# Attention with layer norm: three of the four statistics of a coming group taken in the group's first tile

## The chip, the core and the metric

The kernel runs on one core of one Trainium2 chip. The core has five engines that run side by side and meet only at semaphores: PE (matrix products, the loads of its weights shown apart as PEld), DVE (vector work), ACT (activations and copies), POOL (vector work too), and SP, which here issues the transfers. The metric is the device time of one execution in microseconds (us), lower is better.

## What is computed

A block of a transformer over 8192 rows of 512 numbers, in single precision: layer norm with a modulation, causal linear attention with 16 heads, a gated residual, then a second layer norm with a modulation, a gated feed-forward with 1536 hidden columns, and a gated residual. The change is in the attention half:

```python
h = _layernorm(x) * (1 + ca) + sa          # x is (1, 8192, 512)
qkv = h @ W_qkv + b_qkv                    # q, k, v; 16 heads of 32
q = elu(q * E ** -0.5) + EPS_FEAT
k = elu(k) + EPS_FEAT
kv_s = kv_s + einsum('bhe,bhf->bhef', k_t, v_t)     # per row t, carried on
k_s = k_s + k_t
out_t = einsum('bhe,bhef->bhf', q_t, kv_s) / (einsum('bhe,bhe->bh', q_t, k_s) + EPS_DEN)
x = x + ga * (out @ W_out + b_out)
```

The layer norm needs the mean and the variance of each row of 512.

## The kernel before

Each engine has its own program, written out by hand; the order of the work on an engine is the order of the calls, and every dependency is a wait on a semaphore (`wait`). There is no scheduler. Rows are handled in tiles of 128 and groups of 4 tiles, 16 groups in all. Groups 0 and 1 are written out, groups 2 to 13 run in a loop whose body holds an even and an odd group (`groups`), groups 14 and 15 are written out again. One body works on three groups at once: in group g it computes the attention of the four tiles of g, the projections and features of g + 1, and the layer norm and turning of g + 2.

The program of DVE for groups 0 to 14 is `ahead_of_last`. In it, for each tile t of group g:

- `mask`: four operations that multiply PE's scores in `sc` by the causal mask and write `probs`.
- `feature(n, ...)`: adds the two parts of the feature map (`z_relu`, `z_exp`, from ACT); for a key also a scan, which gives `k_sum`, and a copy of its last column.
- `gate_last`: writes `y`, the gated output product of the tile before, from PE's bank.
- `divide`: numerators from two PSUM banks (`num` and `pj`) times the reciprocal denominators, written to `a_t` in two halves. It releases `a_ready`.
- `norm_stats`, `norm_var`, `norm_x`: the layer norm of group g + 2. `norm_stats` waits for the load of `xg`, 128 rows x 4 tiles x 512, and takes one statistics instruction for each tile; `norm_var` merges them into mean and variance and writes `var_eps`; POOL turns this into `rstd`; `norm_x` normalises `xg` in place.
- `word_size`: only in looped groups; the largest absolute value of a block of feed-forward weights (`most`), merged into `most_of_all` by an operation of one element in each partition.

PE (`front` and `rest`) starts each tile with the scores and three products of 12 matmuls (a product is three passes of four matmuls of 128x512). Two of them wait on semaphores that matter here: in `front`, `wait(pe, a_ready, g * GT + t)` stands in front of the second product of a tile, since that product writes into the bank which `divide` of the tile before reads. The output product (`out_project`, into `sc`) of the tile before follows in `rest`. In group 14 (`near_last`) PE also waits, in `scores` of the second tile, for a flag `wide` that DVE writes behind `divide` of the first tile.

POOL works on the same groups: in tile 1 of a group its queue has `prod_low` (`prod_lo`), a bias add into `x_res`, `rstd_of`, a product `prod` from `k_sum` and `qt`, and the residual add into `x_res`, which waits for `y`. ACT computes the exponentials and the copies. SP loads `xg` of group g + 2 early in group g.

Of the kernel before, what the change touches and what calls it, by code (L numbers as in the profile page):

```python
# [23 lines left out]
GT = 4  # L24
# [24 lines left out]
def wait(eng, sem, value):  # L49

    if not isinstance(value, int) or value > 0:
        eng.wait_ge(sem, value)  # L52
# [127 lines left out]
def attention(nc, s, sem, sbuf, psum, ident, gb_dram, mod_col, half_neg, w_hi, w_lo, xt_hi, xt_lo, ga_row,  # L180
# [100 lines left out]
    def odd_bank(tile, t):  # L281

        if isinstance(tile, int) and tile >= (NG - 1) * GT:
            return turn_bank_of(tile) if t < 3 else sc[:, 0, :]
        return pj[:, (t + 1) % 2, :]
# [554 lines left out]
    def vector(dve, sum_of, low):  # L840
        def norm_stats(g, tiles=range(GT)):
            wait(dve, x_in, 16 * (g + 1))
            for t in tiles:
                ins = dve.bn_stats(stats[:, t, :], xg[:, t, :])
            if tiles[-1] == GT - 1:
                ins.then_inc(ln_chain, 1)

        def norm_var(g):
            wait(dve, ln_chain, 2 * g + 1)
            wait(dve, xn_ready, g)  # L850
            if not isinstance(g, int):
                dve.sem_inc(dve_passed, 1)
            for t in range(GT):
                ins = dve.bn_aggr(mean_var[:, t, :], stats[:, t, :])
            ins.then_inc(ln_chain, 1)
            wait(dve, ln_chain, 2 * g + 2)
            dve.tensor_scalar(var_eps[:, 0:GT], mean_var[:, 0:GT, 1], EPS_LN, None, ALU.add).then_inc(var_ready, 1)
# [21 lines left out]
        def feature(g, parity, n):  # L879

            kind, c = unit_of(n)
            to = (kt, qt)[kind][parity]
            wait(dve, exp_ready, g * 2 * C + n + 1)
            dve.scalar_tensor_tensor(to[:, c, :], z_relu[:, n % 2, :], EPS_FEAT, z_exp[:, n % 2, :],
                                     ALU.add, ALU.add).then_inc(phi_ready, 1)
            if kind == 0:
                wait(dve, phi_ready, g * 2 * C + n + 1)
                wait(dve, prod_ready, g * C + c - 1)
                first = isinstance(g, int) and g == 0
                wait(dve, past_ready, (g - 1) * C + c + 1)  # L890
                dve.tensor_tensor_scan(k_sum[:, c % 2, :], to[:, c, :], to[:, c, :],
                                       0.0 if first else k_past[:, c:c + 1],
                                       ALU.add, ALU.bypass).then_inc(ksum_ready, 1)
                wait(dve, ksum_ready, g * C + c + 1)
                dve.tensor_copy(k_past[:, c:c + 1], k_sum[:, c % 2, GN - 1:GN]).then_inc(past_ready, 1)

        def v_rows(g, parity, t):
            wait(dve, pj_ready, g * UNITS + 2 * C + t + 1)
            dve.tensor_tensor(out=v[parity][:, t, :], in0=pj[:, t % 2, :], in1=bv_row[:, :],
                              op=ALU.add).then_inc(v_ready, 1)  # L900

        def recip(g, parity, c):
            wait(dve, den_ready, g * C + c + 1)
            dve.reciprocal(r_den[parity][:, c, :], r_den[parity][:, c, :]).then_inc(rden_ready, 1)  # L904

        def mask(tile):
            wait(dve, sc_ready, tile + 1)
            for h in range(HPC):
                dve.tensor_tensor(out=probs[:, h, :].rearrange("p (c i) -> p c i", c=C),  # L909
                                  in0=sc[:, h, :].rearrange("p (c i) -> p c i", c=C),  # L910
                                  in1=causal[:, :].rearrange("p (a i) -> p a i", a=1).broadcast_to([P, C, P]),
                                  op=ALU.mult).then_inc(probs_ready, 1)

        def divide(tile, g, parity, t):
            wait(dve, num_ready, tile + 1)
            wait(dve, rden_ready, (g + 1) * C)
            wait(dve, a_lo_ready, tile)
            for odd, bank in enumerate((num, odd_bank(tile, t))):
                ins = dve.tensor_tensor(out=a_t[:, :].rearrange("p (k e i) -> p e k i", e=2, k=2)[:, odd, :, :],  # L919
                                        in0=bank[:, :].rearrange("p (k e i) -> p e k i", e=2, k=2)[:, odd, :, :],  # L920
                                        in1=r_den[parity][:, :, t * P:(t + 1) * P]
                                        .rearrange("p (k e) i -> p e k i", e=2)[:, odd, :, :], op=ALU.mult)
            ins.then_inc(a_ready, 1)

        def gate_y(tile):
            wait(dve, op_ready, tile + 1)
            if isinstance(tile, int) and tile == 0:
                dve.wait_ge(ga_ready, 2)
            wait(dve, y_ready, tile)
            dve.tensor_tensor(out=y[:, :], in0=y_bank_of(tile), in1=ga_row[:, :],  # L930
                              op=ALU.mult).then_inc(y_gated, 1)

        def gate_last(g, t):
            tile = g * GT + t - 1
            if not isinstance(tile, int) or tile >= 0:
                gate_y(tile)

        def word_size(i, slot, words, landed):

            wait(dve, *landed)  # L940
            dve.tensor_reduce(most[:, slot:slot + 1], words.bitcast(I32), AX.X, ALU.max,
                              apply_absolute_value=True).then_inc(most_ready, 1)
            wait(dve, most_ready, i + 2)
            wait(dve, most_merged, i + 1)
            dve.tensor_tensor(out=most_of_all[:, :], in0=most_of_all[:, :], in1=most[:, slot:slot + 1],
                              op=ALU.max).then_inc(most_merged, 1)
# [78 lines left out]
        def ahead_of_last(g, parity):  # L1025
            n = g + 1
            other = 1 - parity
            looped = not isinstance(g, int)
            near_last = isinstance(g, int) and g == NG - 2
            first = isinstance(g, int) and g == 0  # L1030

            mask(g * GT)
            if not first:
                v_rows(g, parity, 3)
                recip(g, parity, 3)
            feature(n, other, 0)
            if first:
                recip(0, 0, 2)
                recip(0, 0, 3)
            feature(n, other, 1)  # L1040
            gate_last(g, 0)
            divide(g * GT, g, parity, 0)
            if near_last:
                dve.wait_ge(beyond_ps, 1)
                dve.tensor_scalar(wide[:, :], x_bank[0:1, 0:1], 0.5, None, ALU.is_gt).then_inc(wide_ready, 1)

            mask(g * GT + 1)
            norm_stats(g + 2)
            norm_var(g + 2)
            feature(n, other, 2)  # L1050
            feature(n, other, 3)
            if looped:
                word_size(g * 3 + (-6), 0, r_den[other][:, 2, :], (unit_in[0], g * 16 + (-16)))
            gate_last(g, 1)
            if looped:
                word_size(g * 3 + (-5), 1, r_den[other][:, 1, :], (down_in, g * 16 + (-16)))
            feature(n, other, 4)
            norm_x(g + 2)
            divide(g * GT + 1, g, parity, 1)

            mask(g * GT + 2)
            feature(n, other, 5)
            recip(n, other, 0)
            feature(n, other, 6)
            xt_low(g + 2, parity, 0)
            feature(n, other, 7)
            gate_last(g, 2)
            if looped:
                word_size(g * 3 + (-4), 2, r_den[other][:, 3, :], (unit_in[1], g * 16 + (-16)))
            divide(g * GT + 2, g, parity, 2)  # L1070
            xt_low(g + 2, parity, 1)

            mask(g * GT + 3)
            v_rows(n, other, 0)
            recip(n, other, 1)
            v_rows(n, other, 1)
            xt_low(g + 2, parity, 2)
            v_rows(n, other, 2)
            if near_last:
                recip(n, other, 2)  # L1080
            gate_last(g, 3)
            if not near_last:
                recip(n, other, 2)
            xt_low(g + 2, parity, 3)
            divide(g * GT + 3, g, parity, 3)

        def group(g, parity):
# [10 lines left out]
            if not last:  # L1098
                return ahead_of_last(g, parity)
# [1103 lines left out]
```

## Time and profile before

| what | us |
|---|---|
| median of 3 runs | 2059.73 |
| lowest and highest run | 2059.23 and 2059.74 |
| the profiled execution | 2060.73 |
| its span | 2059.0 |
| granted clock of PE over the span | 0.998 of full speed |

The rows further down come from the profiled execution. The attention part takes about the first 1050 us of it, a looped group 63 us, a tile 15 to 17 us. All looped groups look alike; group 7, whose four tiles start near 515, 530, 545 and 561 us, is the one from which single rows are read.

### The profile page before, as it was taken

The page shows a single profiled execution, that of the slowest core. Times are in us where ns is not written, and L with a number is a line of the kernel's source. Part 1 is how long each engine was busy: PE and PEld are TensorE (multiplying, and loading weights), DVE is VectorE, ACT ScalarE, POOL GpSimd, SP SyncE. Part 2 cuts the span into 40 slices and gives each one's busy share as a digit, 9 for nine tenths or more (in the row PEclk, how much of TensorE's full clock was granted, in tenths as well). Part 3 has the DMA queues.
Part 4 walks back from the last instruction along what each step waited for, and adds up shares of the span by engine and source line. Part 5 has one row for each costly group of instructions (what it writes and reads, how often), then busy time and mean ns, then how long its engine had stood idle before and what let it go on. Part 6 is the DMA issues. An engine that isn't in the chain of part 4 may idle for free. (4 is left out here: it accounts for less than half of the span.)

```text
span 2059.0 us, 44446 instructions
## 1 busy us (share of the span) xinstructions
PE 2021.3 (98%) x16388; PEld 1645.8 (80%) x16388; DVE 1554.2 (75%) x2228; ACT 1001.7 (49%) x1733; POOL 956.9 (46%) x782
## 2 busy tenths in 40 slices
PE   7999999999999999999999999999999999999998
PEld 4788888888888888888868888888888888878887
DVE  7988988898988899888885755857567575765743
ACT  5444554555544455545453544535464353644533
POOL 2645544555445455444534344443534444344444
PEclk9999999999999999999999999999999999999999
DMA  7111222321222322222266465654646556465453
GB/s 260 32 58 47 79 83 88 98 93 58 90 91 83 99 68 80 85 89 83 73 221 224 150 204 184 204 183 168 194 168 208 179 177 204 143 215 178 163 169 103
DMA packets 157163, 276.80 MB, mean 134 GB/s; under 512 B 11105, under 2 KB 35681, under 8 KB 157026
## 3 DMA queue, kind: packets, MB, share of 16 engines
q1 hardware_dynamic: 156498, 273.73, 40.4%
q8 instruction: 110, 1.80, 0.4%
q10 hardware_dynamic: 528, 1.05, 0.1%
q14 instruction: 27, 0.22, 0.0%
HBM read 208.67 MB, written 66.06 MB: 133 GB/s over the span
## 5 line engine op out<-in xcount | busy, mean ns | idle before, releaser
L1639 POOL TENSOR_TENSOR h_lo<-y_rows,h_hi 128x512 fp32r<-128x512 f32 x192 | 246.6, 1303 | 366.0 <-ACT h_hi L1737 366.0
L904 DVE RECIPROCAL r_den<-r_den 128x512 f32<-128x512 f32 x64 | 213.6, 3340 | 0.4 <-ACT r_den L613 0.4
L437 POOL TENSOR_TENSOR x_res<-y,x_res 128x512 f32<-128x512 f32 x64 | 83.4, 1302 | 224.1 <-DVE y L930 213.6
L909 DVE TENSOR_TENSOR probs<-sc,causal 128x512 f32<-128x512 f32 x256 | 158.4, 680 | 11.6 <-PE sc L1273 11.6
L600 ACT ACTIVATE z_exp<-pj,qk_neg 128x512 f32<-128x512 f32 x128 | 88.0, 687 | 153.3 <-PE pj L1245 145.9
L426 POOL TENSOR_TENSOR a_lo<-a_t,a_hi 128x512 fp32r<-128x512 f32 x60 | 81.4, 1356 | 167.1 <-ACT a_hi L628 167.1
L1245 PE MATMUL pj<-xt_hi,w_hi 128*128 128x512 f32 x512 | 146.0, 407 | 9.8 <-DVE a_t L919 7.5
L2067 PE MATMUL sc<-wd,h_hi 128*128 128x512 f32 x384 | 150.6, 392 | 0.0
L2067 PE MATMUL sc<-wd,h_lo 128*128 128x512 f32 x384 | 149.6, 390 | 0.0
L1852 DVE TENSOR_TENSOR r_den<-pj,k_tok 128x512 f32<-128x512 f32 x96 | 66.3, 690 | 98.6 <-ACT k_tok L1720 52.2
L1245 PE MATMUL pj<-xt_lo,w_hi 128*128 128x512 f32 x512 | 138.6, 392 | 1.8 <-DVE xt_lo L876 1.8
L1245 PE MATMUL pj<-xt_hi,w_lo 128*128 128x512 f32 x512 | 138.6, 393 | 0.0
L1715 ACT ACTIVATE k_tok<-sc 128x512 f32<-128x512 f32 x96 | 56.2, 586 | 158.6 <-PE sc L2010 158.6
L1737 ACT ACTIVATE h_hi<-y_rows 128x512 fp32r<-128x512 f32 x192 | 119.0, 620 | 24.9 <-DVE y_rows L1871 13.4
L421 POOL TENSOR_TENSOR prod_lo<-prod,prod_hi 128x512 fp32r<-128x512 f32 x64 | 84.1, 1314 | 98.6 <-ACT prod_hi L609 98.6
L1245 PEld LDWEIGHTS pj<-xt_hi,w_hi 128*128 128x128 f32 x512 | 92.1, 189 | 36.5 <-DVE a_t L919 13.4
L1710 ACT ACTIVATE kv_diag<-pj 128x512 f32<-128x512 f32 x96 | 57.4, 598 | 123.9 <-PE pj L2010 123.0
L1245 PEld LDWEIGHTS pj<-xt_lo,w_hi 128*128 128x128 f32 x512 | 96.8, 189 | 23.4 <-DVE xt_lo L876 2.2
L1245 PEld LDWEIGHTS pj<-xt_hi,w_lo 128*128 128x128 f32 x512 | 97.1, 190 | 21.1
L1725 ACT ACTIVATE k_sum<-r_den 128x512 f32<-128x512 f32 x96 | 60.7, 632 | 108.3 <-DVE y_rows L1863 95.7
L1863 DVE TENSOR_TENSOR y_rows<-sc,k_sum 128x512 f32<-128x512 f32 x96 | 66.3, 691 | 55.3 <-PE sc L2010 55.1
L1857 DVE TENSOR_TENSOR bv_row<-sc,kv_diag 128x512 f32<-128x512 f32 x96 | 66.3, 691 | 54.9 <-PE sc L2010 54.9
(261 smaller groups left out, 5687.0 us busy)
## 6 DMA issues: line engine op xcount, KB each, us to landing
w_hi<-parts SPq DMA_DIRECT2D x48, 1024.0 KB, 5.3
w_lo<-parts SPq DMA_DIRECT2D x48, 1024.0 KB, 5.3
x_mid<-x_res SPq DMA_DIRECT2D x96, 256.0 KB, 2.6
x_res<-in_L_attn_x SPq DMA_DIRECT2D x64, 256.0 KB, 2.7
xg<-in_L_attn_x SPq DMA_DIRECT2D x15, 1024.0 KB, 6.5
x_res<-x_mid SPq DMA_DIRECT2D x60, 256.0 KB, 4.0
full<-x_mid SPq DMA_DIRECT2D x60, 256.0 KB, 3.6
parts<-r_den SPq DMA_DIRECT2D x48, 256.0 KB, 2.3
```

Of the source, the lines that this page charges most:

```text
L421: pool.tensor_tensor(out=prod_lo[:, :], in0=prod[:, :], in1=prod_hi[:, :].bitcast(F32), op=ALU.subtract).then_inc(prod_lo_ready, 1)
L426: pool.tensor_tensor(out=a_lo[:, :], in0=a_t[:, :], in1=a_hi[:, :].bitcast(F32), op=ALU.subtract).then_inc(a_lo_ready, 1)
L437: pool.tensor_tensor(out=x_res[:, slot, :], in0=y[:, :], in1=x_res[:, slot, :], op=ALU.add).then_inc(y_ready, 1)
L600: act.activation(z_exp[:, n % 2, :], pj[:, n % 2, :], ACT.Relu, bias=qk_neg[:, 1 - kind, c:c + 1], scale=-scale).then_inc(below_ready, 1)
L904: dve.reciprocal(r_den[parity][:, c, :], r_den[parity][:, c, :]).then_inc(rden_ready, 1)
L909: dve.tensor_tensor(out=probs[:, h, :].rearrange("p (c i) -> p c i", c=C), in0=sc[:, h, :].rearrange("p (c i) -> p c i", c=C), in1=causal[ ...
L1245: mm = pe.matmul(to, w[:, k, at:at + P], xt[:, k, :], start=(i == 0), stop=(i == len(passes) - 1))
L1639: pool.tensor_tensor(out=h_lo[b], in0=h[i], in1=h_hi[b].bitcast(F32), op=ALU.subtract).then_inc(h_lo_ready, 1)
L1737: act.activation(h_hi[q % 6 * 2 + i], h[i], ACT.Copy).then_inc(h_hi_ready, 1)
L1852: dve.tensor_tensor(out=c12, in0=sums[1], in1=s12, op=ALU.add).then_inc(c12_ready, 1)
L1857: dve.tensor_tensor(out=c22, in0=xs[q % 2], in1=s5, op=ALU.add).then_inc(c22_ready, 1)
L2067: mm = pe.matmul(dn[i % 4], as_(part[j * 2 + t // GT][:, rows]), as_(wd[half * 6 + j]), start=(j == 0 and part is h_hi), stop=(j == 5 and ...
```

## The change

`norm_stats` is called twice in place of once in groups 1 to 14. The first call takes the statistics of three of the four tiles of group g + 2, and stands between `gate_last` and `divide` of the group's first tile. The second takes the fourth and stands where the whole call stood, behind the mask of the second tile. Both calls wait for the load of `xg`. Group 0 keeps the old order, and so does group 15.

```diff
             feature(n, other, 1)
             gate_last(g, 0)
+            if not first:
+                norm_stats(g + 2, range(3))
             divide(g * GT, g, parity, 0)
             if near_last:
                 dve.wait_ge(beyond_ps, 1)
                 dve.tensor_scalar(wide[:, :], x_bank[0:1, 0:1], 0.5, None, ALU.is_gt).then_inc(wide_ready, 1)
 
             mask(g * GT + 1)
-            norm_stats(g + 2)
+            norm_stats(g + 2, range(0 if first else 3, GT))
             norm_var(g + 2)
```

On DVE, in a looped group, between `y` of tile 0 and the merge of the statistics (rows with L52 are register and semaphore instructions):

```order
-L919 TENSOR_TENSOR a_t<-num,r_den 128x2x128
-L919 TENSOR_TENSOR a_t<-pj,r_den 128x2x128
-L52 REGISTER_ALU
-L909 TENSOR_TENSOR probs<-sc,causal 128x512 x4
-L52 ISA
-L844 BN_STATS stats<-xg 128x6 x4
+L52 ISA
+L844 BN_STATS stats<-xg 128x6 x3
+L919 TENSOR_TENSOR a_t<-num,r_den 128x2x128
+L919 TENSOR_TENSOR a_t<-pj,r_den 128x2x128
+L52 REGISTER_ALU
+L909 TENSOR_TENSOR probs<-sc,causal 128x512 x4
```

Three statistics moved in front of the two halves of the divide and of the four masks; one stays behind the masks.

On DVE in group 14, the written-out group before the last, before the change:

```order
L930 TENSOR_TENSOR y<-sc,ga_row 128x512
L919 TENSOR_TENSOR a_t<-num,r_den 128x2x128
L919 TENSOR_TENSOR a_t<-pj,r_den 128x2x128
L1045 TENSOR_SCALAR wide<-sc 1x1
L909 TENSOR_TENSOR probs<-sc,causal 128x512 x4
L844 BN_STATS stats<-xg 128x6 x4
```

and with it:

```order
L930 TENSOR_TENSOR y<-sc,ga_row 128x512
L844 BN_STATS stats<-xg 128x6 x3
L919 TENSOR_TENSOR a_t<-num,r_den 128x2x128
L919 TENSOR_TENSOR a_t<-pj,r_den 128x2x128
L1047 TENSOR_SCALAR wide<-sc 1x1
L909 TENSOR_TENSOR probs<-sc,causal 128x512 x4
L844 BN_STATS stats<-xg 128x6
```

Here the flag `wide` too stands behind the three statistics. The order on PE, ACT, POOL and SP is the same before and after.

## Rows read from the trace of the kernel before

**Rows 1.** The page, busy time by engine, share of the span, instructions

```profile
PE 2021.3 (98%) x16388; PEld 1645.8 (80%) x16388; DVE 1554.2 (75%) x2228; ACT 1001.7 (49%) x1733; POOL 956.9 (46%) x782
```

**Rows 2.** Waits of PE: first 200 to 950 us, then whole span; total, times, longest

```profile
PE pj L1245 <- DVE a_t L919: 5.4, 12, 0.5
...
PE sc L1273 <- DVE wide L1045: 0.8, 1, 0.8
```

**Rows 3.** Timeline, PE, group 1: start, duration, what, [idle before <- releaser]

```profile
170.61 1.08 PE L1245 MATMUL pj<-xt_hi,w_lo 128*128 128x512 f32 x4
171.53 1.07 PE L1245 MATMUL pj<-xt_hi,w_hi 128*128 128x512 f32 x4
```

**Rows 4.** Timeline, PE and its weight loads, group 7, tile 2

```profile
547.87 1.07 PE L1245 MATMUL pj<-xt_hi,w_lo 128*128 128x512 f32 x4
549.30 0.77 PEld L1245 LDWEIGHTS pj<-xt_hi,w_hi 128*128 128x128 f32 x4 [0.79 <-DVE a_t L919]
549.30 1.21 PE L1245 MATMUL pj<-xt_hi,w_hi 128*128 128x512 f32 x4 [0.36 <-DVE a_t L919]
...
550.35 1.09 PE L1245 MATMUL pj<-xt_lo,w_hi 128*128 128x512 f32 x4
```

**Rows 5.** Timeline, DVE, group 7, tiles 0 and 1

```profile
527.39 0.69 DVE L930 TENSOR_TENSOR y<-sc,ga_row 128x512 f32<-128x512 f32 x1 [0.21 <-PE sc L1332]
529.48 0.42 DVE L919 TENSOR_TENSOR a_t<-num,r_den 128x256 f32<-128x256 f32 x1 [1.39 <-PE pj L1308]
...
530.92 2.48 DVE L909 TENSOR_TENSOR probs<-sc,causal 128x512 f32<-128x512 f32 x4 [0.69 <-PE sc L1273]
533.32 2.46 DVE L844 BATCH_NORM_STATS2 stats<-xg 128x6 f32<-128x512 f32 x4
...
537.48 0.68 DVE L884 SCALAR_TENSOR_TENSOR kt<-z_relu,z_exp 128x512 f32<-128x512 f32 x1
538.20 2.19 DVE L891 TENSOR_TENSOR_SCAN k_sum<-kt,k_past 128x512 f32<-128x512 f32 x1
...
540.52 0.69 DVE L884 SCALAR_TENSOR_TENSOR qt<-z_relu,z_exp 128x512 f32<-128x512 f32 x1
...
541.93 0.67 DVE L945 TENSOR_TENSOR most_of_all<-most_of_all,most 128x1 f32<-128x1 f32 x1
542.52 0.68 DVE L930 TENSOR_TENSOR y<-sc,ga_row 128x512 f32<-128x512 f32 x1
...
543.83 0.82 DVE L945 TENSOR_TENSOR most_of_all<-most_of_all,most 128x1 f32<-128x1 f32 x1
544.57 0.68 DVE L884 SCALAR_TENSOR_TENSOR kt<-z_relu,z_exp 128x512 f32<-128x512 f32 x1
```

**Rows 6.** Timeline, the queue of SP, group 7: the load of `xg` is issued

```profile
518.94 0.38 SPq L300 DMA_DIRECT2D xg<-in_L_attn_x  x1
```

**Rows 7.** Source line 300, the loads of `xg`: us from issue to landing

```profile
DMA to landing us min/median/max: 5.3/6.5/7.6
```

**Rows 8.** Timeline, ACT, group 7, tile 1: an exponential

```profile
535.03 0.63 ACT L604 ACTIVATE z_exp<-z_exp 128x512 f32<-128x512 f32 x1
```

**Rows 9.** Timeline, POOL, group 7, tile 1

```profile
536.25 1.29 POOL L421 TENSOR_TENSOR prod_lo<-prod,prod_hi 128x512 fp32r<-128x512 f32 x1 [2.72 <-ACT prod_hi L609]
537.50 1.81 POOL L431 TENSOR_TENSOR x_res<-x_res,gabo_row 128x512 f32<-128x512 f32 x1
...
541.29 1.29 POOL L416 TENSOR_TENSOR prod<-k_sum,qt 128x512 f32<-128x512 f32 x1
543.35 1.29 POOL L437 TENSOR_TENSOR x_res<-y,x_res 128x512 f32<-128x512 f32 x1 [0.76 <-DVE y L930]
```

**Rows 10.** Source line 891, the scans: duration in ns, minimum/median/maximum

```profile
L891 DVE TENSOR_TENSOR_SCAN k_sum<-kt,k_past x60: 1283/1284/2202, 84.1 to 997.7; 128x512 f32<-128x512 f32 x60
```

**Rows 11.** Timeline, PE, group 7: last pass of the output products, tiles 0 and 1

```profile
526.28 1.07 PE L1332 MATMUL sc<-w_hi,a_lo 128*128 128x512 f32 x4
...
540.92 1.07 PE L1332 MATMUL sc<-w_hi,a_lo 128*128 128x512 f32 x4
```

## The prediction

> **What bounds the kernel now.** I read the page first, then who waited for whom on PE, then a timeline of one group of the attention part. The page has PE busy for 98% of the span and DVE for 75% [rows 1]. PE is the bound, so an edit on DVE only pays where PE waits for DVE. Between 200 and 950 us, which holds twelve trips through a group, the waits of PE have one single row: 12 times, 5.4 us in total, PE waited for `a_t` [rows 2]. It is the same place each time: tile 2 of a group, where the fourth product of the tile reuses the bank that `divide` of tile 1 reads. Groups 0 and 14 have waits of their own, group 1 has none.
>
> The idle time in that row is less than what PE loses. Undisturbed, one pass of four matmuls follows the other after 171.53 - 170.61 = 0.92 us [rows 3]. Around the wait in group 7, two passes take 550.35 - 547.87 = 2.48 us instead of 1.84: 0.64 us lost, where the matmul row reports 0.36 idle and the weight-load row 0.79 [rows 4]. The recorded 1.07 us of a pass overlaps its successor, and the load of the weights can't run ahead across the wait. So the row of 5.4 us is no ceiling for what can be won. The Trainium skill says the same in "Perfetto Trace Analysis", Identifying the Most-Contended Engine: matmul busy time is a bad measure since matmuls are pipelined, and weight loads are the better one. By the matmul rows alone the most that could come back would be 5.4 us; the trace's pitch agrees with the skill.
>
> **What DVE does in tile 1.** Group 7, [rows 5]: from the mask of tile 1 (530.92) on, DVE has no idle time of size until `divide` of tile 1: mask, four statistics (533.32), aggregates, a feature with its scan, a feature, a word-size step, `y` (542.52), a word-size step, a feature (544.57), normalise, divide. The end of that chain releases PE. In tile 0, by contrast, DVE waited 1.39 us in front of the divide and 0.69 us in front of the mask, both for PE [rows 5]. The change carries three statistics from the full tile into the one with idle time.
>
> **Step 1, tile 0.** Four masks step by (533.32 - 530.92)/4 = 0.60 us, and the statistics have the same size and pace: three are 1.80 us. DVE is free from 527.39 + 0.60 = 527.99, the divide started at 529.48: 1.49 us of cover [rows 5]. So the divide of tile 0 comes 0.31 us later. The mask behind it had 0.69 us of idle time, so it still starts when PE's scores are there: cost 0. PE uses this divide only after one more product of three passes, 2.8 us later: cost 0. If that cover were gone, each us of delay beyond 0.38 would go into the mask and from there into the chain of tile 1. ACT and POOL get `a_t` 0.31 us later, ahead of an output product of PE whose last pass starts at 540.92 [rows 11]: cost 0.
>
> The wait on the load of `xg` moves ahead of the divide too. The load is issued at 518.94 and lands at worst 7.6 us later, at 526.5, while DVE gets there at 527.99 [rows 6, 7]: cost 0, with 1.4 us to spare at worst.
>
> **Step 2, tile 1 up to `y`.** DVE is 1.80 us ahead after the one statistic that stays. This doesn't pass through whole. The feature behind the aggregates started at 537.48 [rows 5] and could come at 535.68, but its exponential ends on ACT at 535.03 + 0.63 = 535.66 [rows 8] and reaches DVE some 0.04 us later: 535.70, an even thing. The scan behind it meets POOL. The trace shows that DVE's operations with two inputs in SBUF and POOL's run one after the other: a merge of 128x1 elements took 0.67 us and ended at 542.60, where POOL's product (541.29 + 1.29) ended at 542.58; the next took 0.82 and ended at 544.65, where POOL's residual ended at 544.64 [rows 5, 9]. A scan took 2.19 us behind POOL's bias add (537.50) where the median is 1.28 [rows 5, 9, 10]. So in the new order: POOL's `prod_lo` starts at 536.25 as now (it waits for ACT), the scan gets in when its reads end, about 537.4, and ends near 538.7; POOL's bias add goes in behind the scan, to about 539.8; DVE's second feature gets in near 539.6. From that feature to the merge it is 541.93 - 540.52 = 1.41 us [rows 5], so the merge stands at 541.0. POOL's product stands at 541.3 as now, since POOL's queue from 536.25 has the same work and the same turns with DVE. The merge is first by 0.3 us. Then `y` could start from 541.6, but PE's output product ends at 540.92 + 1.07 = 541.99, and `y` starts 0.04 us after that, as in tile 0 (526.28 + 1.07 = 527.35, then 527.39) [rows 5, 11]: 542.03 instead of 542.52. **Of 1.80 us there remain 0.49.** The gate is PE itself: it can't be less than 542.03, and it is 542.52 or later where the merge falls behind the product.
>
> A rule speaks here. The Trainium skill, "SBUF — State Buffer", Who interferes with whom, has the shared ports of DVE and GpSimd as an exclusive lock, which "issue order, not op shape" decides, taken by DVE operations with two SBUF inputs and not by those with one. By it the moved statistics, which read one tensor, don't meet POOL's residual of tile 0, and the merge is settled by who issues first. The trace agrees on the merges; that statistics pass beside POOL is not shown in the rows here.
>
> **Step 3, from `y` to PE.** POOL's residual starts 543.35 - 542.52 = 0.83 us after `y`, that is at 542.86, after the product has ended (542.58); the merge and the feature stand behind it as now [rows 5, 9]. Everything from `y` to the divide of tile 1 keeps its distance to `y`. So `a_t` is released 0.49 us earlier, and PE, which lost 0.64 us here, gets 0.49 of it and keeps losing 0.15. Group 7 has about the smallest loss of the twelve (0.36 idle, against a mean of 5.4/12 = 0.45), so in the others too the whole 0.49 fits. Nothing else is late next: no other row stands in the view of waits [rows 2], and in tiles 2, 3 and 0 the other engines are paced by PE and move with it.
>
> **Step 4, the ends.** Group 0 keeps its old order. Group 1 has no wait to win. In group 14 (the last before the attention's end) the small `wide` operation stands behind the divide, and PE did wait 0.8 us for it [rows 2]: the divide comes up to 0.31 us later, so PE loses up to 0.3 us once. What follows the attention part moves as it is.
>
> **Sum.** 12 x 0.49 = 5.9 won, 0.3 lost: 5.6 us. The profiled execution took 2060.73 us for a span of 2059.0; the median of the runs is 2059.73, so 1 us lower, and the difference goes on that median: 2059.73 - 5.6 = 2054.1. Bounds: with 0.40 us for each group, 4.5 us, 2055.2; with the whole 0.64, 7.7 - 0.3 = 7.4 us, which the gate at 541.99 speaks against; with 0.52, 5.9 us, 2053.8.
>
> **Rivals.**
> (a) The merge loses to POOL's product. It leads by only 0.3 us, and the estimate of the lock's turns is the weakest link. Then it ends at 542.6 as now, `y` starts at 542.52, nothing is won: 2059.73 + 0.3 = 2060.0. For it: the thin margin. Against it: both times hang on the same bias add, so they slip together; and were POOL's reciprocal root to get in before the feature, the product would start near 540.8, be out of the way at 542.0, and `y` would still be at 542.03. That the change doesn't do what it says (no statistic runs in the idle time) would end at the same time.
> (b) Half of it: DVE comes to `y` some 0.25 us after PE, because one more turn of the lock or a late exponential stands in the way. 12 x 0.25 - 0.3 = 2.7 us: 2057.0.
> (c) Slower: POOL's product is itself pushed back, because the scan and the feature in front take turns with it in another order, and the merge still falls behind it. From a start of the product later than 541.3 on, `y` comes later than now. At 541.65, `y` is at 542.87, 0.35 us later than now: 12 x 0.35 + 0.3 = 4.5 us more, 2064.2. For it: POOL's queue has three operations there that each yield to DVE. Against it: it needs both a slip of POOL and a slip of DVE by more.
>
> **How the numbers follow.** Forecast 68%, (a) 13%, (b) 12%, (c) 7%. Faster by over 0.2% (4.1 us, about what a measurement of this kernel can tell from no change) needs 0.37 us for each group: the forecast and a small part of (b), 70%. Within 0.2%: (a) and the rest of (b), 23%. Slower: 7%. The range of 8 in 10 holds the forecast and (b): from 2053.3, half a us below the 0.52 case for the scatter of a median, to 2057.8.
>
> **What would show it.** In a looped group of the changed kernel: three statistics between `y` and `divide` of tile 0, the divide's idle time gone, the mask of tile 1 still with idle time for PE (about 0.7 us); the small `var_eps` operation at about 0.2 us; the first merge after `y`'s gate no longer stretched and in front of POOL's product; `y` of tile 1 with a short wait for PE's output product; the twelve waits of PE for `a_t` at near zero in the matmul rows but still there in the weight-load rows (about 0.3 to 0.4 us); one group shorter by 0.5 us. Wrong would be: `y` of tile 1 still released by nothing but DVE's own chain, or a stretched merge in front of it; a wait for `xg` in tile 0; a mask of tile 1 without idle time.

## The result, and the profile after

The changed kernel takes 2053.64 us (median of 9 runs, 2053.14 to 2055.01); the kernel before, on the same chip, takes 2059.59 us (9 runs, 2057.8 to 2060.26). The ratio is 0.9972, with a 95% interval of 0.9964 to 0.9981: faster by 5.95 us, or 0.28%. The forecast was 2054.1 us. Two of the experiments further down had one slow execution each, of 5156.45 and 4524.65 us, and their medians and ranges are those of the other executions.

The profiled execution of the changed kernel took 2053.5 us for a span of 2051.8. That is 7.2 us less than the profiled execution of the kernel before (2060.73), which lay about 1 us above its own median. So the traces differ by a little more than the medians do, and what lies outside the twelve looped groups is not read as a gain.

The page's busy line of the changed kernel answers to [rows 1]. PE's busy time has not moved (2021.3 before, 2021.4 now); DVE lost 8.7 us of busy time although it has the same 2228 instructions:

```profile
PE 2021.4 (99%) x16388; PEld 1646.2 (80%) x16388; DVE 1545.5 (75%) x2228; ACT 1002.8 (49%) x1733; POOL 955.4 (47%) x782
```

Next the waits between 200 and 950 us, first of PE's weight loads, then of DVE (engine, what it was about to do, for whom it waited; total us, times, longest). The view of PE's matmuls, where [rows 2] had 5.4 us in 12 waits, holds no row at all any more. The weight loads had waited 10.4 us for `a_t` in the kernel before; now:

```profile
PEld pj L1247 <- DVE a_t L919: 4.5, 12, 0.4
PEld sc L1275 <- DVE y L930: 2.0, 11, 0.2
```

```profile
DVE y L930 <- PE sc L1334: 39.6, 36, 2.2
DVE kt L884 <- ACT z_exp L604: 17.6, 24, 0.9
...
DVE probs L909 <- PE sc L1275: 4.1, 12, 0.4
```

10.4 - 4.5 = 5.9 us less for the weight loads is 0.49 us for each of twelve groups, the number of the prediction. For `y` DVE had waited for PE 23 times in this stretch; it does so 36 times now, one time more in each of the twelve groups (and one elsewhere). These waits are the gate of which Step 2 speaks. The row of `a_t`, 16.1 us before, is gone: the statistics fill it.

DVE in group 7, tiles 0 and 1 of the changed kernel, the answer to [rows 5] (start, duration, engine, line, what it writes from what, idle time before it and who ended it):

```profile
525.06 0.69 DVE L930 TENSOR_TENSOR y<-sc,ga_row 128x512 f32<-128x512 f32 x1 [0.22 <-PE sc L1334]
525.67 1.87 DVE L844 BATCH_NORM_STATS2 stats<-xg 128x6 f32<-128x512 f32 x3
527.45 0.41 DVE L919 TENSOR_TENSOR a_t<-num,r_den 128x256 f32<-128x256 f32 x1
...
528.56 2.48 DVE L909 TENSOR_TENSOR probs<-sc,causal 128x512 f32<-128x512 f32 x4 [0.36 <-PE sc L1275]
530.96 0.68 DVE L844 BATCH_NORM_STATS2 stats<-xg 128x6 f32<-128x512 f32 x1
...
532.24 0.17 DVE L857 TENSOR_SCALAR var_eps<-mean_var 128x4 f32<-128x4 f32 x1
533.30 0.69 DVE L884 SCALAR_TENSOR_TENSOR kt<-z_relu,z_exp 128x512 f32<-128x512 f32 x1 [0.88 <-ACT z_exp L604]
534.02 2.21 DVE L891 TENSOR_TENSOR_SCAN k_sum<-kt,k_past 128x512 f32<-128x512 f32 x1
...
536.36 1.51 DVE L884 SCALAR_TENSOR_TENSOR qt<-z_relu,z_exp 128x512 f32<-128x512 f32 x1
...
538.59 0.16 DVE L945 TENSOR_TENSOR most_of_all<-most_of_all,most 128x1 f32<-128x1 f32 x1
539.64 0.69 DVE L930 TENSOR_TENSOR y<-sc,ga_row 128x512 f32<-128x512 f32 x1 [0.89 <-PE sc L1334]
540.25 0.68 DVE L941 TENSOR_REDUCE most<-r_den 128x1 f32<-128x512 int32 x1
540.96 0.81 DVE L945 TENSOR_TENSOR most_of_all<-most_of_all,most 128x1 f32<-128x1 f32 x1
541.70 0.68 DVE L884 SCALAR_TENSOR_TENSOR kt<-z_relu,z_exp 128x512 f32<-128x512 f32 x1
...
545.63 0.42 DVE L919 TENSOR_TENSOR a_t<-num,r_den 128x256 f32<-128x256 f32 x1
```

Read it from above. Three statistics stand between `y` and the divide of tile 0. The mask still has idle time, so the later divide cost nothing. In tile 1 the feature now waits for its exponential (0.88 us): the small `var_eps` took 0.17 us where it had taken 1.18, so DVE got there 1.0 us earlier than the 1.80 us of moved work alone would bring it, and that surplus ends in this wait. The merge at 538.59 takes 0.16 us where it took 0.67. Then DVE is idle for 0.89 us until PE has finished the output product. From `y` to the divide it is 545.63 - 539.64 = 5.99 us; before it was 548.50 - 542.52 = 5.98, so the rest kept its distance.

POOL in the same place, the answer to [rows 9]:

```profile
533.86 1.29 POOL L421 TENSOR_TENSOR prod_lo<-prod,prod_hi 128x512 fp32r<-128x512 f32 x1 [2.38 <-ACT prod_hi L609]
535.11 2.22 POOL L431 TENSOR_TENSOR x_res<-x_res,gabo_row 128x512 f32<-128x512 f32 x1
...
538.73 1.29 POOL L416 TENSOR_TENSOR prod<-k_sum,qt 128x512 f32<-128x512 f32 x1
540.48 1.28 POOL L437 TENSOR_TENSOR x_res<-y,x_res 128x512 f32<-128x512 f32 x1 [0.45 <-DVE y L930]
```

And PE with its weight loads, the answer to [rows 4] and [rows 11]:

```profile
538.53 1.07 PE L1334 MATMUL sc<-w_hi,a_lo 128*128 128x512 f32 x4
...
545.44 1.08 PE L1247 MATMUL pj<-xt_hi,w_lo 128*128 128x512 f32 x4
546.43 1.20 PE L1247 MATMUL pj<-xt_hi,w_hi 128*128 128x512 f32 x4
547.46 1.08 PE L1247 MATMUL pj<-xt_lo,w_hi 128*128 128x512 f32 x4
```

```profile
546.43 0.76 PEld L1247 LDWEIGHTS pj<-xt_hi,w_hi 128*128 128x128 f32 x4 [0.33 <-DVE a_t L919]
```

The output product ends at 538.53 + 1.07 = 539.60 and `y` starts at 539.64. The merge (538.59) started 0.14 us before POOL's product (538.73). The two passes around the wait take 547.46 - 545.44 = 2.02 us, where they took 2.48 and would take 1.84 undisturbed: 0.46 us came back in this group and 0.18 are still lost, though the matmul row shows no idle time.

Over eleven whole groups (from the last pass before the transposes in tile 2 of group 2 to the same pass of group 13) PE took 929.11 - 236.38 = 692.73 us before and 923.53 - 235.63 = 687.90 now. That is 0.44 us for each group, or 5.3 us for twelve. The difference of the medians is 5.95; the fastest and slowest runs of one kernel lie 1.9 to 2.5 us apart, so 0.6 us between the two readings says nothing.

### The profile page after: what moved, and what is told of

Its sections match the earlier page's. It is cut to its first block and busy times, and to the rows that moved or that the text cites. A ratio compares the mean times of both kernels' runs of the same rounds, so it can differ in the third digit from the quotient of the medians.

```text
span 2051.8 us, 44446 instructions
## 1 busy us (share of the span) xinstructions
PE 2021.4 (99%) x16388; PEld 1646.2 (80%) x16388; DVE 1545.5 (75%) x2228; ACT 1002.8 (49%) x1733; POOL 955.4 (47%) x782
```

## Experiments

The theory is the one of the prediction: what is won per group is set by the end of PE's output product, not by how far DVE is ahead, and DVE is freed of a long merge because it now meets the lock it shares with POOL at another moment. The rivals are that the gain grows with the work taken out of tile 1, and that the moved statistics rather than the merge give it. Each run's ratio is against the kernel before on the same chip, whose median was 2059.41, 2059.39 and 2059.08 us in the three groups of runs. One number from group 7 tells the kernels that have the gain from those without it, and I call it the **lag**: from the end of PE's output product in tile 1 to the start of the divide of tile 1. In the kernel before it is 548.50 - 541.99 = 6.51 us, in the changed one 545.63 - 539.60 = 6.03.

### One statistic moved in place of three

```diff
-                norm_stats(g + 2, range(3))
+                norm_stats(g + 2, range(1))
...
-            norm_stats(g + 2, range(0 if first else 3, GT))
+            norm_stats(g + 2, range(0 if first else 1, GT))
```

> Only one of the four statistics is taken in tile 0, three stay in tile 1. Theory G (the gate): what comes through to PE is fixed by y of tile 1, which can't start before PE's output product of tile 0 has ended; 0.6 us of lead is enough to reach that gate, because POOL's bias add sets when the second feature runs, and the merge still gets in front of POOL's product. So the gain is that of the change, about 5.5 to 6 us, near 2053.8 us where the kernel before has 2059.6, and y of tile 1 waits for PE in the looped groups. Rival P (in proportion): what counts is how much DVE time leaves tile 1, so a third of it brings a third of the gain, 2 us, 2057.6 us. The divide of tile 0 is not delayed at all here (0.6 us of work in 1.4 us of idle time), so group 14 loses nothing.

Measured 2052.44 us (2051.6 to 2053.15), ratio 0.9965, 0.9952 to 0.9977: all of the gain with a third of the move. It is 1.2 us below the changed kernel, and 0.6 below its repeat. The flag of group 14 (`wide`), for which PE waits 0.8 us here and 1.0 us there, accounts for 0.2 us of that; for the rest the intervals overlap. DVE waits for the gate here too, 0.66 us:

```profile
537.74 0.16 DVE L945 TENSOR_TENSOR most_of_all<-most_of_all,most 128x1 f32<-128x1 f32 x1
538.57 0.69 DVE L930 TENSOR_TENSOR y<-sc,ga_row 128x512 f32<-128x512 f32 x1 [0.66 <-PE sc L1334]
```

The weight loads wait for `a_t` 4.6 us in 12 times, as in the changed kernel (4.5). That the gain is in proportion to what is moved is false.

### All four statistics moved

```diff
-                norm_stats(g + 2, range(3))
+                norm_stats(g + 2, range(GT))
...
-            norm_stats(g + 2, range(0 if first else 3, GT))
+            if first:
+                norm_stats(g + 2)
```

> All four statistics in tile 0. The divide of tile 0 comes 0.9 us later than in the kernel before, the mask of tile 1 0.2 us later. Theory G: y of tile 1 is at PE's gate all the same, no change against three moved; group 14 pays 0.6 us more for its flag: 2053.6 to 2054.6 us. Rival P (in proportion to the statistics moved): a third more gain than with three, 2051.6 us.

Measured 2054.4 us (2053.76 to 2056.77), ratio 0.9978, 0.9968 to 0.9987. The weight loads wait 4.4 us in 12 times. The fourth statistic brings nothing, as the gate says, and in group 14 PE waits 1.6 us for `wide` instead of 1.0, the 0.6 us that had been expected.

### No statistic moved, only the merge made cheap

From the kernel before. In tile 1 the merge, with two inputs in SBUF, is replaced by a copy with one input; the running maximum is thereby not carried on.

```diff
             wait(dve, most_merged, i + 1)
+            if slot == 0:
+                dve.tensor_copy(most_of_all[:, :], most[:, 0:1]).then_inc(most_merged, 1)
+                return
```

> The kernel before, all four statistics in tile 1; in the first word-size step of tile 1 the merge (a maximum of two one-element tensors in SBUF) is replaced by a copy of one element, so the largest value is not carried on from before that block. The number and place of the DVE instructions is the same. Theory G with the lock: in the kernel before y of tile 1 was late only because that merge, with two inputs in SBUF, stood behind POOL's product. The copy of one element takes 0.15 us beside POOL (as those of k_past do), y starts at PE's gate, 0.49 us earlier, and the whole gain of the change appears without any statistic moved: 2053.6 to 2054.5 us. Rival S: what helped was DVE time taken out of tile 1; here none is taken out, so the time is that of the kernel before, 2059.5 us.

Measured 2053.72 us (2051.78 to 2053.95), ratio 0.997, 0.9959 to 0.9981. This is the run that settles what the merge was worth. DVE in group 7:

```profile
537.80 0.68 DVE L941 TENSOR_REDUCE most<-r_den 128x1 f32<-128x512 int32 x1
538.60 0.15 DVE L946 COPY most_of_all<-most 128x1 f32<-128x1 f32 x1
538.70 0.69 DVE L930 TENSOR_TENSOR y<-sc,ga_row 128x512 f32<-128x512 f32 x1
```

and POOL at the same moment:

```profile
537.96 1.29 POOL L416 TENSOR_TENSOR prod<-k_sum,qt 128x512 f32<-128x512 f32 x1
```

POOL's product is running when the copy comes (537.96 to 539.25), exactly where a merge was held until the end. The copy passes in 0.15 us and `y` starts at 538.70; the output product had ended at 537.59 + 1.07 = 538.66. With all four statistics in tile 1, the whole gain is there. So in the kernel before DVE reached the gate in time already, with nothing to spare: here `y` starts without idle time in front of it, 0.04 us behind the product. It was one operation of 128x1 elements, held until POOL's product ended, that cost 0.49 us per group. What moving the statistics does is to bring this merge in front of POOL's product. That it is the moved work as such that pays is false.

### More work in tile 0: two and four further statistics

From the changed kernel, in looped groups, with results that nothing reads (`range(2)` here, `range(4)` in the second run):

```diff
                 norm_stats(g + 2, range(3))
+                if looped:
+                    for more in range(2):
+                        dve.bn_stats(stats[:, GT + more, :], xg[:, more, :])
```

> The changed kernel with two more statistics (of tiles 0 and 1 again, into unused slots) in front of the divide of tile 0 in the looped groups: 1.2 us more DVE work in tile 0. Theory G: the mask of tile 1 starts 0.8 us later (1.2 less the 0.36 us that it still waited), which only takes up the 0.88 us that the feature in tile 1 waits for ACT: the same time as the changed kernel, 2053.6 us, at most 0.5 us above. Rival L: DVE is filled up, its work in tile 0 counts once the idle time in front of the divide is gone: 12 x 0.8 = 10 us more, 2063 us.

> The same with four more statistics, 2.4 us more DVE work in tile 0. Theory G: a_t of tile 0 comes 2.4 us later, POOL's a_lo and first product with it, so prod_lo starts some 0.8 us late, and the turns behind it (scan, bias add, feature, merge) shift by as much; y of tile 1, which had 0.89 us of wait, comes up to 0.4 us late: 0 to 5 us more than the changed kernel, 2053.6 to 2058.6 us. Rival L: 12 x 2.0 = 24 us more, 2078 us.

With two more: 2053.44 us (2051.69 to 2054.01), ratio 0.997, 0.9957 to 0.9983. The mask's idle time is gone, the feature's idle time has shrunk to nothing, `y` still waits 0.90 us for PE. 1.2 us of further work on DVE cost nothing measurable.

With four more: 2059.3 us (2058.4 to 2061.2), ratio 1.0002, 0.9993 to 1.0011. The whole gain is gone, and more than I had allowed (up to 5 us; it is 5.7 against 2053.64 and 6.3 against the repeat of the changed kernel). The waits of PE between 200 and 950 us read as those of [rows 2] again:

```profile
PE pj L1250 <- DVE a_t L919: 5.3, 12, 0.5
```

I had thought that `y` would be up to 0.4 us late. It is not: the output product ends at 539.54 + 1.07 = 540.61, and `y` follows at once. DVE and then POOL in group 7:

```profile
540.56 0.16 DVE L945 TENSOR_TENSOR most_of_all<-most_of_all,most 128x1 f32<-128x1 f32 x1
540.66 0.69 DVE L930 TENSOR_TENSOR y<-sc,ga_row 128x512 f32<-128x512 f32 x1
541.27 0.68 DVE L941 TENSOR_REDUCE most<-r_den 128x1 f32<-128x512 int32 x1
541.98 1.24 DVE L945 TENSOR_TENSOR most_of_all<-most_of_all,most 128x1 f32<-128x1 f32 x1
543.15 0.68 DVE L884 SCALAR_TENSOR_TENSOR kt<-z_relu,z_exp 128x512 f32<-128x512 f32 x1
```

```profile
532.32 1.30 POOL L426 TENSOR_TENSOR a_lo<-a_t,a_hi 128x512 fp32r<-128x512 f32 x1 [4.13 <-ACT a_hi L628]
...
540.70 1.27 POOL L416 TENSOR_TENSOR prod<-k_sum,qt 128x512 f32<-128x512 f32 x1
541.93 1.28 POOL L437 TENSOR_TENSOR x_res<-y,x_res 128x512 f32<-128x512 f32 x1
```

The late divide of tile 0 makes POOL late (`a_lo` at 532.32), and POOL's queue stays late up to the product at 540.70. The residual can't follow `y` but follows the product, at 541.93, and the second merge (541.98) comes 0.05 us behind it and is held until it ends, at 543.21. It takes 1.24 us. In the changed kernel the residual (540.48) had run for 0.48 of its 1.28 us when that merge came (540.96), and the merge took 0.81. The lag is 547.08 - 540.61 = 6.47 us, nearly the 6.51 of the kernel before. So there is a second place with the same mechanism as the first, behind `y`: the merge is 0.43 us longer than in the changed kernel, and the lag 0.44. The cover in tile 0 that Step 1 speaks of does end somewhere between two and four further statistics, but the cost comes by way of POOL.

### What stands ahead of the gate, and what behind it

From the changed kernel, in looped groups, the word-size step ahead of `y` is left out (`no_size` keeps its waits and signals), so one block of weights is missing from the largest value; in the second run the step behind `y` is left out instead.

```diff
-                word_size(g * 3 + (-6), 0, r_den[other][:, 2, :], (unit_in[0], g * 16 + (-16)))
+                no_size((unit_in[0], g * 16 + (-16)))
             gate_last(g, 1)
```

```diff
-                word_size(g * 3 + (-5), 1, r_den[other][:, 1, :], (down_in, g * 16 + (-16)))
+                no_size((down_in, g * 16 + (-16)))
             feature(n, other, 4)
```

> The changed kernel, but in the looped groups the first word-size step of tile 1 (a reduce and a merge of one element) is left out; it stands in front of y. Its two semaphores are still counted up. So the largest weight value is not taken over that block. Theory G: y of tile 1 already waits 0.89 us for PE, 1.4 us less work in front of it only makes that wait longer, 2.3 us, and the time stays at that of the changed kernel, 2053.6 us. Rival L (load): any DVE work taken out of tile 1 gives PE the rest of what it loses there, 12 x 0.2 to 0.3 us, so 2050.5 us, as in the run with the step behind y left out.

> The changed kernel, but in the looped groups the second word-size step of tile 1, which stands directly behind y, is left out in the same way (its block is not counted in the largest value). Theory G: behind the gate every piece of DVE work counts; a_t is released some 1.4 us earlier and the waits of PE's weight loads for it (4.5 us in total over twelve groups in the changed kernel) vanish. PE gets back 12 x 0.2 to 0.3 us: 2050.2 to 2051.2 us. If nothing changes against the changed kernel, the remaining loss has another cause.

Ahead: 2053.73 us (2052.58 to 2054.43), ratio 0.997, 0.9959 to 0.9982. Nothing is won; the wait of `y` grows from 0.89 to 1.77 us. I had expected 2.3 us, with 1.4 us for the step; from the start of its reduce to the end of its merge the step takes only 538.75 - 537.80 = 0.95 us.

```profile
539.00 0.69 DVE L930 TENSOR_TENSOR y<-sc,ga_row 128x512 f32<-128x512 f32 x1 [1.77 <-PE sc L1339]
```

Behind: 2049.55 us (2048.69 to 2051.19), ratio 0.9952, 0.9939 to 0.9965, and no wait of the weight loads for `a_t` is left. `y` starts at 536.73, 0.04 us behind the output product, so the lag is 542.17 - 536.69 = 5.48 us. This is the sharpest statement of the gate: the same kind of work is worth nothing ahead of `y` and 4.2 us behind it (2053.73 and 2049.55, on the same chip). That is more than the 2.4 to 3.4 us that I had expected. What PE still lost in the changed kernel accounts for some 3 of them: 0.18 us in group 7, 0.27 in group 2, an even one, where the weight loads wait 0.42 us instead of 0.33, and a little where scores wait for `y`. Where the last one comes from, I can't show.

The divide came less early than expected too: the step took 541.70 - 540.25 = 1.45 us, but the lag shrank by 0.55. The scan behind `y` lost the rest. It now starts while POOL's residual runs, and takes 2.19 us where it took 1.28 in the changed kernel; the residual took 1.60 instead of 1.28:

```profile
538.06 2.19 DVE L891 TENSOR_TENSOR_SCAN k_sum<-kt,k_past 128x512 f32<-128x512 f32 x1
```

```profile
537.57 1.60 POOL L437 TENSOR_TENSOR x_res<-y,x_res 128x512 f32<-128x512 f32 x1 [0.46 <-DVE y L930]
```

So work behind the gate isn't worth its full length in lag where its going lets another operation meet POOL. It was enough here because PE lost only 0.18 to 0.27 us a group.

### Both word-size steps ahead of the gate

Nothing is left out here; the step behind `y` is done ahead of it, in the time in which DVE waits anyway.

```diff
-            gate_last(g, 1)
             if looped:
                 word_size(g * 3 + (-5), 1, r_den[other][:, 1, :], (down_in, g * 16 + (-16)))
+            gate_last(g, 1)
```

> The changed kernel, and in the looped groups both word-size steps of tile 1 stand in front of y, nothing left out. Theory G: the second step now runs while DVE waited for PE (0.89 us). Its merge meets POOL's product and ends near the product's end, so y starts about 0.4 us later than now, which PE's next scores can bear (2 us away), but the work behind y is 1.4 us shorter, so a_t comes 0.9 to 1.1 us earlier and PE loses nothing there any more: 2050.2 to 2051.2 us, faster than the changed kernel by 2.5 to 3 us. Rival Y: the later y holds PE's scores or POOL's residual, and the time is that of the changed kernel or above, 2053.6 to 2056 us.

> The kernel with three statistics moved and both word-size steps in front of y, once more, on the chip of this batch: 2050.4 us, to compare the two.

Measured 2050.41 us (2050.14 to 2051.46), ratio 0.9957, 0.9944 to 0.997, and with another group of runs 2049.91 (2049.03 to 2050.58), ratio 0.9953, 0.994 to 0.9967. It beats both kernels: 2.6 to 3.7 us less than the changed one, depending on which medians are compared. PE in group 7 at the place of the wait:

```profile
543.22 1.08 PE L1246 MATMUL pj<-xt_hi,w_lo 128*128 128x512 f32 x4
544.14 1.08 PE L1246 MATMUL pj<-xt_hi,w_hi 128*128 128x512 f32 x4
545.06 1.08 PE L1246 MATMUL pj<-xt_lo,w_hi 128*128 128x512 f32 x4
```

The passes follow each other after 0.92 us: nothing is lost. DVE:

```profile
537.16 0.65 DVE L945 TENSOR_TENSOR most_of_all<-most_of_all,most 128x1 f32<-128x1 f32 x1
537.73 0.68 DVE L930 TENSOR_TENSOR y<-sc,ga_row 128x512 f32<-128x512 f32 x1
...
543.16 0.42 DVE L919 TENSOR_TENSOR a_t<-num,r_den 128x256 f32<-128x256 f32 x1
```

`y` is 0.36 us behind the end of the output product (536.30 + 1.07 = 537.37), but the divide is only 5.79 us behind it, 0.24 less than in the changed kernel, and not the 0.9 to 1.1 us that I had expected: the scan behind `y` took 2.19 us here as well, beside POOL's residual. The time came out as forecast although this size did not, since 0.24 us less lag is about all that PE was losing. Eleven groups take 919.44 - 234.72 = 684.72 us.

### The same with one statistic moved

```diff
-                norm_stats(g + 2, range(3))
+                norm_stats(g + 2, range(1))
```

and the second call from 1 on, with both word-size steps ahead of `y` as above.

> One statistic in tile 0, three in tile 1, and both word-size steps of tile 1 in front of y in the looped groups; nothing left out. Theory G: as the run with the two word-size steps in front, PE no longer waits for a_t in the looped groups; and the flag of group 14 is not delayed (0.2 us): 2050.2 us, between 2049.2 and 2050.8, at least as fast as the same with three statistics moved. Rival: with 1.2 us less lead y comes later than PE's gate by more than PE can bear and a part of the waits is back: 2051 to 2053 us.

Measured 2053.49 us (2051.86 to 2054.84), ratio 0.9971, 0.996 to 0.9982: a miss, 3.3 us above what I had expected. DVE:

```profile
539.40 0.68 DVE L930 TENSOR_TENSOR y<-sc,ga_row 128x512 f32<-128x512 f32 x1
...
544.83 0.41 DVE L919 TENSOR_TENSOR a_t<-num,r_den 128x256 f32<-128x256 f32 x1
```

`y` starts 0.56 us behind the end of the output product (537.77 + 1.07 = 538.84) without idle time in front: DVE's own chain sets it, with a merge in it that POOL holds: the second one takes 0.65 us and ends at 538.83 + 0.65 = 539.48, where POOL's product ends at 538.17 + 1.29 = 539.46. That product starts 0.67 us ahead of the end of the output product, where with three statistics moved it was 0.87, and `y` is later by the same 0.20 us. The lag is 5.99 us, and the weight loads wait 3.8 us for `a_t`. As soon as enough work stands ahead of the gate, the gate no longer binds, and when DVE and POOL get there counts again. There, three statistics are worth 3.6 us more than one (2049.91 and 2053.49, on the same chip), while in the place of the changed kernel they are worth nothing more.

### The changed kernel again

> The changed kernel itself, unchanged, beside the kernels of this batch: 2053.6 us as before (2053.0 to 2054.3), so that differences of one or two us between kernels can be read on one chip.

2053.03 us (2052.11 to 2054.77), ratio 0.997, 0.9959 to 0.9982; eleven groups take 922.31 - 234.86 = 687.45 us, 0.48 us less per group than before.

### All of them by their lag

| kernel | lag in group 7, us | weight loads wait for `a_t`, 200 to 950 us | median, us |
|---|---|---|---|
| before | 6.51 | 10.4 | 2059.59 |
| four further statistics | 6.47 | 10.4 | 2059.3 |
| changed | 6.03 | 4.5 | 2053.64 |
| changed, again | 6.02 | 4.5 | 2053.03 |
| four moved | 6.03 | 4.4 | 2054.4 |
| two further statistics | 6.02 | 4.6 | 2053.44 |
| merge as a copy | 6.03 | 4.6 | 2053.72 |
| size ahead left out | 6.02 | 4.6 | 2053.73 |
| one moved | 6.02 | 4.6 | 2052.44 |
| one moved, sizes first | 5.99 | 3.8 | 2053.49 |
| sizes first | 5.79 | none | 2050.41 |
| sizes first, again | 5.78 | none | 2049.91 |
| size behind left out | 5.48 | none | 2049.55 |

The seven rows at 6.02 and 6.03 us take 2052.44 to 2054.4 us. Their waits for `wide` in group 14 account for up to 0.8 us of that; the rest isn't ordered by the lag.

## Why the prediction was right, step by step

**What bounds the kernel.** Right: PE's busy time is unchanged, and the time came back where PE waited for `a_t`. That the idle time of the matmul rows understates the loss was right too: after the change they show none, while 0.18 us are still lost in group 7 and 4 us more came back when the step behind `y` was left out. The size of the gain alone doesn't show it: 5.9 us by the weight loads and 5.3 by the lengths of the groups lie on either side of the 5.4 us of idle time.

**Step 1.** Right. The mask's idle time went from 0.69 to 0.36 us (0.38 in the step). Nothing waited for `xg`. Two more statistics cost nothing either; the cover ends before four. The list of what would show it named 0.7 us for this idle time, against the step itself; that line was wrong.

**Step 2.** The gate and its size are right: `y` starts 0.04 us behind the end of the output product, and 0.49 of 1.80 us pass. The way there was roughly right. Relative to the start of `prod_lo`, the merge came at 4.73 us (4.75 in the step) and POOL's product at 4.87 (5.04). So the lead of the merge was 0.14 us, not 0.3: the product's start was the term mis-sized, because the bias add and the reciprocal root took other turns with DVE than I had assumed (from its start to the next start the bias add took 2.17 us where it had taken 1.77, the root 1.45 instead of 2.02). The margin on which rival (a) hung was real and thinner than written. The copy shows its price directly: with the merge held, 2059.39 us; with a copy that isn't held, 2053.72. That `y` would wait for PE is right as well, but 0.89 us is no short wait. The step let `y` start from 541.6 if PE allowed it, which makes 0.43 us of wait; it had given the free merge 0.6 us, and that merge takes 0.16. The step also left out that `var_eps` would no longer be held, though the list of signs names its 0.2 us; the wait for the exponential took that up.

The rule of the Trainium skill ("SBUF — State Buffer", Who interferes with whom) that operations of DVE with at most one SBUF input, outside the modes with two ports, don't contend with GpSimd was open then. The trace agrees with it: three statistics ran in 1.87 us from 525.67 on, the pace of 0.60 us each, beside POOL's residual add from 525.89 on for 1.28 us, and the copy took 0.15 us beside POOL's product.

**Step 3.** Right. POOL's residual came 0.84 us after `y` (0.83 in the step), the way from `y` to the divide is 5.99 against 5.98 us, and the weight loads' waits fell by 0.49 us per group. PE keeps losing 0.18 us in group 7 (0.15 in the step). The length of the groups gives 0.44, not 0.49. Part of the difference is in the other row of the weight loads, the scores that wait for `y` (10 waits, 1.7 us before; 11 and 2.0 us now); "nothing else is late next" was a little too strong.

**Step 4.** Right in kind. In group 14 PE's wait for `wide` grew from 0.8 to 1.0 us over the whole span, 0.2 us where up to 0.3 was written:

```profile
PE sc L1275 <- DVE wide L1047: 1.0, 1, 1.0
```

**Sum.** 5.6 us forecast, 5.95 measured between the medians, 12 x 0.44 - 0.2 = 5.1 by the lengths of the groups; they lie within 0.9 us of each other, less than the runs of one kernel scatter. The forecast of 2054.1 us is 0.5 us from the median. Of the rivals none came about, but (a) did in the run with four further statistics, at another merge than the one named.

## What to carry to other kernels

Where an engine's chain comes to its last wait for the bounding engine with time to spare, work taken out ahead of that wait brought nothing here, and work taken out behind it did: find this gate, read how much idle time stands in front of it, and put what can't be avoided ahead of it, but no more than fits. Then look at what meets whom afterwards, since a step of 1.45 us taken out brought only 0.55 where the next operation ran into POOL. Look also for tiny operations with a long duration: the one that took 0.67 us where its like takes 0.16 was held by another engine, and changing its form brought as much here as moving 1.80 us of real work. And where PE waits, count passes from start to start, or the waits of the weight loads, since the idle time of the matmul rows can read zero while 0.18 us per group are still lost.

## What the runs showed of the hardware

- The merge of 128x1 elements with two inputs in SBUF took 0.65, 0.67, 0.81 or 1.24 us in group 7 of these kernels when it came while POOL was in an operation of 128x512 elements, and each time it ended as that one ended. It took 0.16 us while POOL was in the small `rstd` (128x4 elements, 1.48 us by the profile), so a long span on POOL doesn't hold it by itself. A copy of 128x1 took 0.15 us in the middle of a large operation. So DVE and POOL meet not only at semaphores: an operation of one can hold up one of the other with no wait between them in the program.
- `var_eps`, a tensor-scalar operation of 128x4 elements with one tensor as input, was held too: in the kernel with the copy it took 1.16 us and ended at 533.07 + 1.16 = 534.23, where POOL's `prod_lo` ended at 532.91 + 1.29 = 534.20; with all four statistics moved it took 0.61 us and ended at 531.16, where POOL's product ended at 531.13; in the changed kernel it comes while POOL waits, and takes 0.17 us. I didn't test it apart. The Trainium skill names a case that it could be ("SBUF — State Buffer", Who interferes with whom): such operations can enter a mode with two ports, and then contend.
- Time in which DVE is held counts as busy. The 8.7 us of busy time that DVE lost are twelve times what three operations changed in group 7: `var_eps` 1.0 us less, the merge 0.5 less, the feature `qt` 0.8 more (1.51 instead of 0.69), 8.4 together.
- A wait that the weight loads show as 0.79 us cost PE 0.64, and one of 0.33 us cost 0.18: 0.15 less both times.
